# A selective scan on four engines: the order and classes of its sixteen states

## The reference, cut to what matters

```python
def step(h, inputs):
    dt_t, x_t, B_t, C_t = inputs
    h = jnp.exp(dt_t[..., None] * A) * h + (dt_t * x_t)[..., None] * B_t[:, None, :]
    y = jnp.einsum('bds,bs->bd', h, C_t)
    return (h, y)
...
y = jnp.swapaxes(ys, 0, 1) + x * D
y = y * silu(z)
```

## Time and profile before

| | us |
|---|---|
| median of 3 runs | 3788.19 (3787.15 to 3791.84) |
| the profiled execution | 3791.31 |
| its span | 3789.5 |
| PE busy in the span | 3250.4 |
| VectorE busy | 2505.3 |
| ScalarE busy | 1842.0 |
| GpSimd busy | 1374.3 |
| mean granted clock of PE | 0.941 of full speed |

### The profile page before, as it was taken

One profiled execution on the slowest core, in us unless ns is written; L12 is line 12 of the kernel. 1 busy time (PEld: TensorE's weight loads), 2 busy tenths in 40 slices (PEclk: granted clock), 3 DMA queues, 4 the chain that ended last, 5 costly groups with the idle time before them and its releaser, 6 DMA issues. The chain is left out here.

```text
span 3789.5 us, 52272 instructions
## 1 busy us (share of the span) xinstructions
PE 3250.4 (86%) x18096; PEld 1982.8 (52%) x18096; DVE 2505.3 (66%) x4630; ACT 1842.0 (49%) x3956; POOL 1374.3 (36%) x904
## 2 busy tenths in 40 slices
PE   8599999669999799799999799798388888888894
PEld 4244444346666555466666455343155656566773
DVE  8488887357777522277777332398599999996533
ACT  2177788335555411165555211256377777772100
POOL 4100000222222211122222111134599999995403
PEclk9699999889999999899999899899699999999897
DMA  5946662520000131200000321244525151514573
GB/s 166 149 52 72 72 72 31 155 88 22 22 22 22 35 124 51 68 18 22 22 22 20 88 74 45 77 142 146 215 85 195 56 195 67 198 48 150 177 218 114
DMA packets 282801, 342.63 MB, mean 90 GB/s; under 512 B 71556, under 2 KB 217836, under 8 KB 281900
## 3 DMA queue, kind: packets, MB, share of 16 engines
q1 hardware_dynamic: 268732, 315.54, 30.3%
q10 hardware_dynamic: 10736, 15.38, 1.2%
q0 software_dynamic: 3072, 8.39, 0.7%
HBM read 231.21 MB, written 107.48 MB: 89 GB/s over the span
## 5 line engine op out<-in xcount | busy, mean ns | idle before, releaser
L2348 POOL TENSOR_TENSOR H_feed<-H_ndu,H_bs 128x1024 f32<-128x1024 f32 x256 | 595.6, 2373 | 5.5 <-DMA H_bs<-between_bc 2.9
L709 ACT ACTIVATE B_probs<-B_p_exp,B_key_bias 128x512 f32<-128x512 f32 (+3 forms) x768 | 393.6, 582 | 108.3 <-PE B_p_exp L753 78.2
L643 DVE TENSOR_REDUCE B_part_max<-B_p_max 128x1 f32<-128x512 f32 (+3 forms) x768 | 375.4, 546 | 92.9 <-PE B_p_max L730 90.3
L1239 ACT ACTIVATE D_probs<-D_scores,D_neg,D_rq 128x256 f32<-128x256 f32 x512 | 283.0, 573 | 265.8 <-DVE D_neg L1148 265.8
L2319 ACT ACTIVATE H_decay<-H_ndt,H_rate 128x1024 f32<-128x1024 f32 x256 | 287.9, 1125 | 197.6 <-DVE H_turning L2401 102.3
L1087 POOL TENSOR_TENSOR D_rnorm<-D_norm,D_power 128x8 f32<-128x8 f32 x64 | 106.2, 1659 | 582.4 <-DVE D_norm L1103 582.4
L727 PE MATMUL B_p_max<-B_k,B_q 100*128 100x512 bf16 (+3 forms) x768 | 256.3, 340 | 39.9 <-DMA B_key_bias<-in_key_bias 34.0
L1652 PE MATMUL E_p_ag<-E_hT,E_w 128*128 128x512 f32 x640 | 283.8, 603 | 2.1 <-ACT E_hT L1608 2.1
L2401 DVE TENSOR_TENSOR_SCAN H_turning<-H_decay,H_feed 128x1024 f32<-128x1024 f32 x112 | 253.4, 2274 | 23.0 <-POOL H_feed L2348 22.9
L2452 PEld LDWEIGHTS H_p_y<-H_minus,H_sT 128*128 128x128 f32 x1792 | 224.0, 199 | 75.9 <-ACT H_sT L2304 56.1
L2452 PE MATMUL H_p_y<-H_minus,H_sT 128*128 128x128 f32 x1792 | 232.4, 286 | 35.8 <-ACT H_sT L2304 35.8
(11 more groups left out here) (263 smaller groups left out, 6922.3 us busy)
## 6 DMA issues: line engine op xcount, KB each, us to landing
H_bs<-between_bc SPq DMA_DIRECT2D x64, 512.0 KB, 7.3
H_cs<-between_bc SPq DMA_DIRECT2D x36, 512.0 KB, 7.8
B_q<-between_q_parts SPq DMA_DIRECT2D x96, 128.0 KB
B_k<-between_k_parts SPq DMA_DIRECT2D x96, 128.0 KB
D_base<-between_z SPq DMA_DIRECT2D x64, 128.0 KB
between_z<-D_z SPq DMA_DIRECT2D x64, 128.0 KB, 1.7
E_rest<-between_z SPq DMA_DIRECT2D x16, 512.0 KB, 5.1
between_sz<-F_sz SPq DMA_DIRECT2D x8, 1024.0 KB, 4.2
```

Source lines behind the costliest of these rows:

```text
L643: nc.vector.reduce_max(part_max[:, g % 2, kc, qb, h:h + 1], p_max[:, n % 3, 0:keys], AX.X).then_inc(maxed, 1)
L709: nc.scalar.activation(probs[:, x % PROBS, skip:512], p_exp[:, n % SCORES, skip:512], ACT.Exp, bias=key_bias[:, g % SETS, kb - 4 * Q + 4, ...
L1239: last = nc.scalar.activation(probs[:, place[m], :, :].rearrange("p a b -> p (a b)"), scores[:, place[m], :, :].rearrange("p a b -> p (a b ...
L2348: nc.gpsimd.tensor_tensor(feed[:, n % AHEAD, :], ndu[:, g % 2, :], bs[:, s, :], ALU.mult).then_inc(fed, 1)
```

## The change

The string that gives each state its class is another one. The counts go from seven T, six D and three P to eight T, six D and two P, and most classes stand at other states:

```diff
@@ -2156,7 +2156,7 @@
         tiles = [(i, m) for i in range(SEQS) for m in range(XT)]
         units = [(g, s) for g in range(len(tiles)) for s in range(NS)]
         NU = len(units)
-        CLASS = "TTDPTDTDPTDTPDTD"
+        CLASS = "TTDTPTDTDTPTDDTD"
         NB = SEQ // P
         HB = NB // 2
         NEXT_C = CLASS.index("P", NS // 2)
```

## The result

The changed kernel is slower: its time stands to that of before as 1.0034, 95% interval 1.0024 to 1.0044, which on the median of before in the same runs, 3787.63 us, is +12.9 us (9.1 to 16.7). The median of ten runs is 3799.70 us (3795.39 to 3806.33); the forecast was 3797.7. In a few executions the chip is in a slower state (one of the eleven here took 5781.98 us), and all medians and ratios in this document are of the others. The profiled execution took 3797.80 us with a span of 3796.0.

What follows compares the result with a forecast made beforehand. GpSimd with VectorE behind it was taken to set the 45.19 us tile. Per tile -0.89 + 1.43 + 0.10 = +0.64 us, over 15 tiles +9.6, first tile -0.1: +9.5 on 3788.19 gives 3797.7 us, range 3786 to 3805.

Steps and rivals of the forecast that it cites:

- the loop of GpSimd and VectorE: Scan before the change: each waits once per tile for the other, setting 45.19 us; VectorE's 0.89 us wait would go.
- The turn of state 3 starts at 13.08 us of the tile: PE's queue: the turn stands behind the addition of state 2, 1.7 us late; scan 6 loses 1.43 us.
- State 9 adds 0.10: PE's turn of state 9 waits behind additions, so scan 12 starts at 32.98 instead of 32.88 us (bounds 0 and 0.6).
- The terms of an ordinary tile: Each tile after the first: -0.89 + 1.43 + 0.10 = +0.64 us.
- the two holds: Late turns of states 3 and 9 on PE delay scans 6 and 12, by 1.43 and 0.10 us per tile.
- The tile of 45.8: Scan stage: a tile was to take 45.8 us, forecast range 45.6 to 46.1, against 45.19 before.
- the hold doesn't reach VectorE: Rival, chance 0.12: scan 6 starts by 15.6 us of the tile, leaving about -14 us, 3774.
- loss and gain cancel: Rival: a hold of 1.0 us, no gain per tile, 3788 to 3792; chance 0.12 together with GpSimd as bound.
- GpSimd stays the bound: Rival: product of state 10 is late, tile stays at 45.2 us; chance 0.12 together with cancelling.
- The clock: Rival, chance 0.11: PE's granted clock drops in the start of the tile, 3805 to 3815 us.
- gaps of PE of at most 1.3 us: PE's idle gaps in the new order, shorter than one before a clock fall, so falls were expected to get fewer.
- The rule of strict order: PE: matmuls start and end in program order, so state 3's transposes can't pass the addition; otherwise the first rival's sum.

Runs made afterwards that it cites:

- Experiment 5: Kernel before, with GpSimd's product of state 12 made on 8 of its 1024 columns; ratio 0.9960, 3772.43 us.
- Experiment 1: Changed kernel, with PE's turn of state 3 ahead of the addition of state 2; ratio 0.9985, 3782.47 us.
- experiment 10: Changed kernel, with the turns of states 3 and 9 ahead of the additions of states 2 and 8, C turned at 10; ratio 0.9967, 3773.83 us.
- experiment 6: Changed kernel, with GpSimd's product of state 10 made twice in each tile; ratio 1.0093, 3823.93 us.
- experiment 2: Changed kernel, with the classes of states 3 and 4 exchanged (P at 3, T at 4); ratio 1.0069, 3814.75 us.
- experiment 9: Changed kernel, with the turns of states 3 and 9 ahead and C turned at state 12 instead of 10; ratio 0.9984, 3779.98 us.

## Why the prediction was right

- **What bounds the kernel before**: the loop of GpSimd and VectorE with 0.89 us of waiting per tile. Experiment 5 took it away and gained 12.7 us in the stage, 15 x 0.85.
- **The turn of state 3 starts at 13.08 us of the tile**: measured 3050.55 - 3037.47 = 13.08. Copies at 13.80, exponential of state 6 at 15.81 (15.82 predicted), scan 6 at 17.01 (17.02). All handovers were taken from rows; the one from ScalarE to VectorE, from another phase, held. Experiment 1 shows that the order is the cause: with the turn ahead, scan 6 starts at 15.60 (15.59 predicted).
- **State 9 adds 0.10**: scan 12 starts 0.14 us late in the trace (3070.44, where 3070.30 would do). Moving its turn ahead as well (experiment 10 against 1) took the tile from 44.51 to 44.22, so the hold of state 9 is worth 0.29 where state 3 holds nothing, and part of it hides behind the hold of state 3 in the changed kernel.
- **The terms of an ordinary tile**: -0.89 for the loop with GpSimd against -0.97 measured (45.19 to 44.22, experiment 10), and 1.43 + 0.10 for the two holds against 1.55 (44.22 to 45.77, the changed kernel). The sum was +0.64 and is +0.58.
- **The tile of 45.8**: 45.77 in nine of 14. The mean is 45.96, and here a term was missing: C's turn at state 10 and its followers, 3 x 0.69 us; two more tiles took 0.28 more by a late start on ScalarE. The stage was to take 9.5 us more and took 11.9: 14 tiles 10.7 (9.0 predicted), the last tile 1.0 (0.6), the first 0.2 (-0.1). That the total comes as near as this is in part luck: the missing 2.6 us are offset by 0.8 us from an ordinary tile that is 0.06 cheaper than predicted.
- **The rivals**: that the hold doesn't reach VectorE is refuted by 24.4 us of its waits for ScalarE. That loss and gain cancel needed a hold of 1.0 us; scan 6 starts 1.41 us late. That GpSimd stays the bound is refuted by its 4.2 us of idle time per tile (3 to 4 predicted) and by experiment 6. The clock did not fall at the start of tiles: it was 1.00 in the first 13.4 us of all 15 tiles after the first, and from 2760 to 3400 its mean rose from 0.98 to 1.00. Here the outcome was right and the reason was weak. I took gaps of PE of at most 1.3 us for too short to bring a fall, and in experiment 1 the clock fell behind gaps of 0.97 and 0.56 us.
- **The rule of strict order** on PE (the Trainium skill, "TensorE: Matmul & The Clock Gate", part on packing, "The mechanism"): by it matmuls start and end in their order in the queue, while a weight load can be pulled ahead of matmuls in flight. The trace agrees. The turn never started before the addition queued ahead of it was through; its first weight load, at 3050.12, came 0.43 us ahead of its first matmul, while the addition was still running.

## What to carry to other kernels

Count for each in-order queue not only how much work it has in a period but what stands in front of the item that somebody waits for; here 1.7 us of a product that nobody was waiting for cost 1.3 us per tile in a queue with 14% idle time. A change of mix and a change of order that come together should be tried apart: the mix was worth 12 to 14 us, the order cost 26. When a hold is moved away from one place, follow the queue for a whole period before claiming the gain, since the next place can be worse (experiment 2).

## What the runs showed that I had not expected

Moving a small step (eight 16-column transposes for C, under 1 us) from state 10 to state 12 cost 4.5 us in the stage, though two D states follow there; two falls of the clock, which came behind that step two times of three, account for 3.2 of them. Before the change the clock fell in the second half of seven of 14 tiles and none of them was longer for it; in experiment 9 a fall cost 1.6 or 1.7 us. And the price of exchanging two letters, 15.8 us between the changed kernel and experiment 2, was larger than that of the whole change.
